# Delta-rule scan of a hybrid layer: key pairs of the state side by side, output terms in two operations a half, the last scan opened for the old block's tiles

## The chip, the cores and the metric

One core of a Trainium2 chip runs the whole kernel. The metric is the device time of one execution in microseconds, the median of several; lower is better.

## The reference

Input x is (2, 1024, 256) in float32. Four sublayers follow each other, each added to its input; LN is a layer norm without weights:

```
x = x + window_attention(LN(x))     # 32 heads of 8, window 128: own and previous block of 128
x = x + ffn(LN(x))                  # 256 -> 1024 relu -> 256, 4-bit weights with scales, plus LoRA
x = x + delta_layer(LN(x))          # below
x = x + ffn(LN(x))                  # the same weights
```

delta_layer, cut to what matters (T = 1024 steps, 32 heads of 8, S is 8 x 8 per head and batch):

```
h = rms(x)
q, k, v = silu(silu(causal_conv4(h @ W.T)))   ; q, k = l2norm(q), l2norm(k) ; beta = sigmoid(h @ Wbeta.T)
for t:  err = S k_t - v_t ;  S = S - beta_t * err k_t^T ;  o_t = S q_t
x = x + rms(o) @ Wout.T ;  x = x + (silu(gate) * up) @ Wdown.T
```

## The kernel before

The 1024 steps are cut into NB = 8 blocks of W = 128 tokens, both batches together. Every engine runs an instruction stream written out by hand as `body(t)` for t = -1 to 8, and waits on semaphores for the others. body(t) holds three blocks at once: the attention, first feed-forward and the delta layer's projections of block n = t+1 (`following`), the scan of block t (`has_scan`), and the tail of block s = t-1 (`tail`: gate_up, mlp_down, ffn_c). `front` is preparation of block n+1 (its queries, keys and score maxima). body(0) has no tail, body(6) no front, body(7) only scan and tail, body(8) only a tail.

**The scan** (VectorE, `scan`, L1180 to L1215). The two batches, 32 heads and two halves of the value rows lie on the 128 partitions; each holds VR = 4 value rows and DK = 8 keys. The block's 128 steps are NC_ = 32 chunks of C = 4. A chunk is four dependent instructions: L1189 multiplies the state by the prepared rows `til` into `first` (a view of `lane_buf`), L1196 sums it to the four steps' updates `u_l`, L1201 multiplies those by the keys into `state[c]`, L1208 sums these products and the old state to the next one. `state` is [NC_+1, VR, DK, C+1]: per value row and key four products and then the state, so states of neighbouring keys lie five floats apart. `between` puts other work of VectorE (score maxima, L1005; attention output scaling, L1037) between the four. The list CUTS has 20, 23 and 24: chunks 0 to 19 run under the attention, 20 to 22 after the second group of maxima, 23 after `first_residual`, and 24 to 31 two at a time after act_of(0) to act_of(3).

**Before the scan** `til_first`, `pair_scale` and `til_column` prepare `til` on VectorE; on GpSimd `pair_rows` (L574) copies the query-key products into `mm_` and `values_til` (L584) the values into `first`; the scan waits for both.

**The output terms** (`terms_of`, L333). o = S q at the start of the chunk plus the chunk's own updates: per step 8 products of state and query and 4 of `mm_` and `u_l`, summed over 12. For 16 chunks that is, for each of four steps, four multiplies by value row (L339) and one for the updates (L340). GpSimd does the first half in `first_terms`, released by the semaphore `scanned`, which VectorE raises after chunk 21, when the room in `lane_buf` is free; VectorE sums them (`first_sums`, L1219), does the second half in `second_terms` between act_of(4) and act_of(5), and sums again (`second_sums`). Then SyncE sends `o_l` to DRAM and back in another layout (L427, L433), ScalarE squares it, TensorE sums the squares, and `output_norm`, `output_product` and `y_of` (L1248) follow.

**Beside it.** On VectorE `first_residual` (L1046), `first_apply` (L986, two scalings of tok), `act_of` (L1256, gate times up, read from PSUM), `second_residual` (L1059, waits for TensorE's ffn_down, L1450), `third_residual` (L1262, waits for mlp_down, L1712), `third_apply`. act_of(i) frees the PSUM tile of gate_up(i+2) (L1703). TensorE runs, per pair, two tiles of ffn_up (L1630) and one of gate_up. ScalarE, in order: 32 exps of the scores (L697), at u=4 the copy of the pair products, at u=16 the copy of attention rows (L705), turn_a(1), y_scale, values_out, turn_c(1) (L663), the norm's root norm_a(1) (L642), a table load, gates 0 to 2 (L816), then relu_a (L743) and the other gates. GpSimd, in order: pair_rows, values_til, first_terms, ffn_bias (L554), ffn_bias_c (L566), residual (L560).

## Time and profile before

| what | value |
|---|---|
| three runs | 1278.09, 1280.63, 1340.21 us; median 1280.63 |
| profiled execution, its own time | 1278.25 us |
| its span, first to last instruction | 1276.4 us |
| mean granted TensorE clock | 0.908 |
| TensorE busy (matmul) | 1060.3 us, 83% |
| VectorE busy | 944.5 us, 74% |
| ScalarE busy | 497.4 us, 39% |
| GpSimd busy | 181.4 us, 14% |
| chain that ended last | TensorE 41%, VectorE 37%, ScalarE 8% |

Busy time is that of executed instructions; waits, semaphores and DMA issues are not in it. The chain is followed back from the last instruction to what released each one. Times in the rows are us from the span's start unless marked ns. A 0.02 to 0.1 us step between two dependent instructions is the semaphore's.

### The profile page before, as it was taken

Reading aid. Unit: us, or ns where it says so; the run is one execution under the profiler, and the core shown is the slowest. Engines: PE = TensorE matmul, PEld = TensorE weight load, DVE = VectorE, ACT = ScalarE, POOL = GpSimd, SP = SyncE. Lnnn points to the kernel's source line nnn. Section 1 sums busy time; section 2 is a strip of 40 time slices with the busy share of each in tenths; the row PEclk is TensorE's granted clock in tenths of the full one; section 3 lists DMA queues with packets and bytes.
Section 4 is the critical chain, followed back from the end, with each engine's and each line's share of the span. In section 5 each row is a group of like instructions: output and inputs, shape, how many; then the busy total and the mean of one; then the engine's idle time right before and its main releaser. Section 6 shows DMA issues by size and latency. Waiting matters only on the chain.

```text
span 1276.4 us, 22025 instructions
## 1 busy us (share of the span) xinstructions
PE 1060.3 (83%) x8600; PEld 723.6 (57%) x8600; DVE 944.5 (74%) x2425; ACT 497.4 (39%) x1027; POOL 181.4 (14%) x251
## 2 busy tenths in 40 slices
PE   3699778777988999989988998899989889932587
PEld 2356545455556755766566655675566547721465
DVE  3824268897889788987888788977897789779611
ACT  2044254326443644345432653364335443610122
POOL 2000000130122010401040013100040004003100
PEclk9579879978998999989988999999999989975788
DMA  9724023203420143013311242024201300110000
GB/s 288 141 46 72 10 75 76 41 1 100 77 41 1 50 111 63 1 34 95 76 21 33 76 82 35 1 75 101 48 2 32 88 2 1 34 58 0 16 9 9
DMA packets 93608, 67.69 MB, mean 53 GB/s; under 512 B 47233, under 2 KB 86337, under 8 KB 93505
## 3 DMA queue, kind: packets, MB, share of 16 engines
q1 hardware_dynamic: 88544, 60.75, 20.1%
q10 hardware_dynamic: 4960, 5.54, 1.6%
q8 instruction: 68, 1.11, 0.4%
q14 instruction: 36, 0.29, 0.1%
HBM read 45.55 MB, written 20.32 MB: 52 GB/s over the span
## 4 chain that ended last, share of the span: by engine, by line
PE 41%; DVE 37%; ACT 8%; DMA 4%; issue 4%; SPq 4%; POOL 1%; DVEq 0%; ACTq 0%; POOLq 0%
PE bank L1558 7%; DVE lane_buf L1189 5%; PE bank L1509 4%; PE bank L1538 4%; DVE state L1208 4%; PE bank L1712 4%; DVE state L1201 4%; DVE u_l L1196 4%; PE bank L1655 3%; PE bank L1543 3%; PE bank L1504 3%; DVE lane_buf L339 2%; DMA q_l<-lane_q 2%; PE bank L1450 2%; DVE mx L1005 2%
## 5 line engine op out<-in xcount | busy, mean ns | idle before, releaser
L697 ACT ACTIVATE probs<-bank 128x512 f32<-128x512 f32 x256 | 152.1, 597 | 200.1 <-PE bank L1543 199.7
L1558 PE MATMUL bank<-probs,v_ext 128*9 128x128 f32 x2048 | 162.0, 279 | 12.1 <-ACT probs L697 6.7
L1005 DVE TENSOR_REDUCE mx<-bank 128x2 f32<-128x320 f32 x256 | 120.9, 486 | 54.3 <-PE bank L1509 49.4
L1703 PE MATMUL bank<-feat_c,wgu 128*128 128x256 f32 (+1 forms) x384 | 96.3, 402 | 57.2 <-DVE hid_c L1256 51.6
L339 POOL TENSOR_TENSOR lane_buf<-state,q_l 128x128 f32<-128x128 f32 x128 | 86.4, 704 | 353.9 <-DVEq L1214 353.9
L1189 DVE TENSOR_TENSOR lane_buf<-state,til 128x128 f32<-128x128 f32 x256 | 109.6, 428 | 17.1 <-POOL lane_buf L584 10.2
L1703 PEld LDWEIGHTS bank<-feat_c,wgu 128*128 128x128 f32 (+1 forms) x384 | 71.1, 190 | 78.1 <-DVE hid_c L1256 55.7
L1558 PEld LDWEIGHTS bank<-probs,v_ext 128*9 128x9 f32 x2048 | 83.5, 91 | 55.1 <-issue 20.3
L1504 PE MATMUL bank<-edge_mask,identb 128*128 128x64 bf16 x512 | 63.1, 208 | 49.8 <-DVE mx L1005 37.6
L1538 PE MATMUL bank<-tri_mask,identb 128*128 128x512 bf16 x256 | 102.1, 399 | 0.5 <-DMA q_stack<-m_rows 0.5
L1543 PE MATMUL bank<-q_stack,k_stack 128*128 128x128 bf16 x1024 | 101.8, 223 | 0.0
L1543 PEld LDWEIGHTS bank<-q_stack,k_stack 128*128 128x128 bf16 x1024 | 81.1, 100 | 33.7 <-issue 4.0
L1509 PE MATMUL bank<-k_stack,q_stack 128*32 128x160 bf16 x2048 | 92.3, 263 | 0.0
L1504 PEld LDWEIGHTS bank<-edge_mask,identb 128*128 128x128 bf16 x512 | 32.8, 101 | 100.3 <-DVE mx L1005 59.7
L1208 DVE TENSOR_REDUCE state<-state 128x32 f32<-128x160 f32 x256 | 81.9, 320 | 7.4
L1196 DVE TENSOR_REDUCE u_l<-lane_buf 128x16 f32<-128x144 f32 x256 | 77.3, 302 | 7.7
L1201 DVE TENSOR_TENSOR state<-u_l,k_l 128x128 f32<-128x128 f32 x256 | 74.8, 292 | 7.2
L1630 PE MATMUL bank<-feat,w_up 128*128 128x256 f32 x256 | 65.6, 406 | 5.4 <-ACT feat L659 5.4
L1726 PE MATMUL bank<-feat_c,w_up 128*128 128x256 f32 x256 | 65.0, 404 | 5.1 <-ACT hid_c L824 3.8
L1083 DVE SCALAR_TENSOR_TENSOR conv<-raw,conv_w,conv 128x256 f32<-128x256 f32 x144 | 63.4, 482 | 2.6
L1726 PEld LDWEIGHTS bank<-feat_c,w_up 128*128 128x128 f32 x256 | 49.6, 201 | 20.7 <-ACT hid_c L824 6.2
L1450 PE MATMUL bank<-w_dn,hid 128*128 128x256 f32 x256 | 57.4, 382 | 4.5 <-ACT hid L743 4.5
(167 smaller groups left out, 1766.1 us busy)
## 6 DMA issues: line engine op xcount, KB each, us to landing
k_pieces<-conv SPq DMA_DIRECT2D x48, 128.0 KB, 2.3
k_stack<-k_pieces SPq DMA_DIRECT2D x32, 192.0 KB
k_stack<-k_pieces SPq DMA_DIRECT2D x32, 128.0 KB
k_l<-lane_k SPq DMA_DIRECT2D x8, 512.0 KB, 3.6
q_l<-lane_q SPq DMA_DIRECT2D x8, 512.0 KB, 5.6
q_pieces<-conv SPq DMA_DIRECT2D x24, 128.0 KB, 2.0
q_stack<-q_pieces SPq DMA_DIRECT2D x32, 96.0 KB
tok<-in_x SPq DMA_DIRECT2D x8, 256.0 KB, 3.2
```

The costliest lines, as they stand in the source:

```text
L697: act.activation(probs[:, u % 2], score_bank[u % 2][:], ACT.Exp, scale=float(DK) ** -0.5).then_inc(exp_done, 1)
L1005: dve.tensor_reduce(mx[:, g, 2 * v:2 * v + 2], bank[1 + u % 2][:, 0:2 * SPAN].rearrange("p (h k) -> p h k", h=2), AX.X, ALU.max).then_inc( ...
L1189: at = mark(dve.tensor_tensor(first[:, c, :, :, 0:DK], state[:, c, :, :, C].rearrange("p v (o k) -> p v o k", o=1).broadcast_to([128, VR, ...
L1196: at = mark(dve.tensor_reduce(u_l[:, c], first[:, c], AX.X, ALU.add))
L1201: at = mark(dve.tensor_tensor(state[:, c, :, :, 0:C], u_l[:, c].rearrange("p v (o i) -> p v o i", o=1).broadcast_to([128, VR, DK, C]), kc[ ...
L1208: at = mark(dve.tensor_reduce(state[:, c + 1, :, :, C], state[:, c], AX.X, ALU.add))
L1504: pe.matmul(edges[:, :, e * W:e * W + SUB], identb[:], edge_mask[:, e * SUB:(e + 1) * SUB].rearrange("p (o s) -> p o s", o=1) .broadcast_t ...
L1509: last = pe.matmul(pb[s * SUB:(s + 1) * SUB, hp * SPAN:(hp + 1) * SPAN], q_stack[:, r, 2 * v + hp, s * SUB:(s + 1) * SUB], keys_of(r, 2 * ...
L1538: pe.matmul(pb[:], identb[:], tri_mask[:].rearrange("p (o t) -> p o t", o=1) .broadcast_to([128, 2, 2 * W]), start=True, stop=False, skip_ ...
L1543: last = pe.matmul(pb[:, at:at + W], keys_of(r, 2 * v + hp)[:, kb * W:(kb + 1) * W], q_stack[:, r, 2 * v + hp, :], start=False, stop=True, ...
L1558: last = pe.matmul(bank[5][row:row + VE, col:col + W], v_ext[:, b, kb, h, :], probs[:, u % 2, (hp * 2 + kb) * W:(hp * 2 + kb + 1) * W], st ...
L1703: last = pe.matmul(late_bank[i % 2][0:m, g * BT:(g + 1) * BT], wgu[:, k, g * INTER + 128 * i:g * INTER + 128 * i + m], fc[:, k], start=(k ...
```

## The change

It lays two keys' groups of the state beside each other (`state` [NC_+1, VR, DK/2, 10]: four products, two states, four products), so that the states of a key pair are neighbours; the four scan instructions keep their sizes, the first one's loops are reordered. `mm_` becomes chunk-major. ScalarE gets two new jobs a block: the queries turned into step-major order (`queries_out`, after exp 16 of the following attention, into the room of `sqk`), and the states of each half copied out densely into `til` (`states_out`: the first half ahead of norm_a(1), the second ahead of gate 5). The output terms of a half become `step_terms` (1024 elements) and `state_terms` (2048): on GpSimd for the first half, on VectorE for the second. `scanned` is raised twice a block. For body(7) VectorE gets `last_scan`, in which act_of, third_residual and third_apply of the old block come between chunks.

```diff
-        mm_ = sb("mm_", [128, C, C, NC_])
+        mm_ = sb("mm_", [128, NC_, C, C])
...
-        state = sb("state", [128, NC_ + 1, VR, DK, C + 1])
-
-        out_terms = lane_buf[:, 0:VR * W // 2 * (DK + C)].rearrange("p (v c i e) -> p v c i e", v=VR, i=C, e=DK + C)
+        state = sb("state", [128, NC_ + 1, VR, DK // 2, 2 * (C + 1)])
+
+        out_terms = lane_buf[:, 0:VR * W // 2 * (DK + C)].rearrange("p (c v i e) -> p c v i e", v=VR, i=C, e=DK + C)
+        q_t = sqk[:].rearrange("p s x -> p (s x)").rearrange("p (c i k) -> p c i k", i=C, k=DK)
+        s_t = til[:].rearrange("p c i k -> p (c i k)").rearrange("p (a x) -> p a x", a=2)[
+            :, :, 0:NC_ // 2 * VR * DK].rearrange("p a (c v k) -> p a c v k", v=VR, k=DK)
...
-        def terms_of(engine, cs, steps=range(C)):
-
-            qc = q_l[:].rearrange("p k (c i) -> p i c k", i=C)
-            n_c = cs.stop - cs.start
-            for i in steps:
-                for v in range(VR):
-                    engine.tensor_tensor(out_terms[:, v, :, i, 0:DK], state[:, cs, v, :, C], qc[:, i, cs, :], ALU.mult)
-                last = engine.tensor_tensor(
-                    out_terms[:, :, :, i, DK:DK + C],
-                    mm_[:, i, :, cs].rearrange("p j (o c) -> p o c j", o=1).broadcast_to([128, VR, n_c, C]),
-                    u_l[:, cs].rearrange("p c v j -> p v c j"), ALU.mult)
-            return last
+        def step_terms(engine, half):
+
+            cs = slice(half * NC_ // 2, (half + 1) * NC_ // 2)
+            return engine.tensor_tensor(
+                out_terms[:, :, :, :, DK:DK + C],
+                mm_[:, cs].rearrange("p c (o i) j -> p c o i j", o=1).broadcast_to([128, NC_ // 2, VR, C, C]),
+                u_l[:, cs].rearrange("p c v (o j) -> p c v o j", o=1).broadcast_to([128, NC_ // 2, VR, C, C]), ALU.mult)
+
+        def state_terms(engine, half):
+
+            cs = slice(half * NC_ // 2, (half + 1) * NC_ // 2)
+            return engine.tensor_tensor(
+                out_terms[:, :, :, :, 0:DK],
+                s_t[:, half].rearrange("p c v (o k) -> p c v o k", o=1).broadcast_to([128, NC_ // 2, VR, C, DK]),
+                q_t[:, cs].rearrange("p c (o i) k -> p c o i k", o=1).broadcast_to([128, NC_ // 2, VR, C, DK]), ALU.mult)
...
-                pool.wait_ge(scanned, n + 1)
-                terms_of(pool, slice(0, NC_ // 2)).then_inc(terms_ready, 1)
+                pool.wait_ge(scanned, n * 2 + 1)
+                step_terms(pool, 0)
+                pool.wait_ge(q_turned, n + 1)
+                pool.wait_ge(s_copied, n * 2 + 1)
+                state_terms(pool, 0).then_inc(terms_ready, 1)
...
-                    last = pool.tensor_copy(mm_[:, i, 0:i + 1, :], pair_l[:, at:at + i + 1, :])
+                    last = pool.tensor_copy(mm_[:, :, i, 0:i + 1].rearrange("p c j -> p j c"), pair_l[:, at:at + i + 1, :])
...
+
+            def queries_out(n, front):
+
+                act.wait_ge(til_ready, n + 1)
+                if front:
+                    act.wait_ge(turned_next, n + 3)
+                act.copy(q_t.rearrange("p c i k -> p k (c i)"), q_l[:]).then_inc(q_turned, 1)
+
+            def states_out(n, half):
+                act.wait_ge(scanned, n * 2 + half + 1)
+                act.copy(s_t[:, half].rearrange("p c v (k e) -> p (c v k) e", e=2),
+                         state[:, half * NC_ // 2:(half + 1) * NC_ // 2, :, :, C:C + 2].rearrange("p c v k e -> p (c v k) e")
+                         ).then_inc(s_copied, 1)
...
+                    if u == QUERIES_AT and after_p:
+                        queries_out(n - 1, front)
...
                 if tail:
                     turn_c(s, 1)
                 if following:
+                    if scan:
+                        states_out(t, 0)
                     norm_a(n, 1)
...
+                if scan and not following:
+                    queries_out(t, False)
...
+                    if following and scan and pair == IT - 4:
+                        states_out(t, 1)
                     if tail and pair < IT - 3:
                         gate_of(s, 3 + pair)
...
+                elif scan:
+                    late(0)
+                    late(1)
+                    states_out(t, 0)
+                    for i in range(2, FT):
+                        late(i)
+                    states_out(t, 1)
...
-                done(dve.tensor_copy(state[:, 0, :, :, C], state[:, NC_, :, :, C]))
+                done(dve.tensor_copy(state[:, 0, :, :, C:C + 2], state[:, NC_, :, :, C:C + 2]))
...
+            def products_of(c):
+
+                whole = state[:, c]
+                return bass.AP(whole.tensor, whole.offset,
+                               [list(whole.ap[0]), [2 * (C + 1) * DK // 2, VR], [2 * (C + 1), DK // 2], [C + 2, 2], [1, C]])
...
                     at = mark(dve.tensor_tensor(
-                        first[:, c, :, :, 0:DK],
-                        state[:, c, :, :, C].rearrange("p v (o k) -> p v o k", o=1).broadcast_to([128, VR, C, DK]),
-                        til[:, c:c + 1, :, 0:DK].broadcast_to([128, VR, C, DK]), ALU.mult))
+                        first[:, c, :, :, 0:DK].rearrange("p v i (k e) -> p i v k e", e=2),
+                        state[:, c, :, :, C:C + 2].rearrange("p v k (o e) -> p o v k e", o=1)
+                        .broadcast_to([128, C, VR, DK // 2, 2]),
+                        til[:, c, :, 0:DK].rearrange("p i (o k e) -> p i o k e", o=1, e=2)
+                        .broadcast_to([128, C, VR, DK // 2, 2]), ALU.mult))
...
                     at = mark(dve.tensor_tensor(
-                        state[:, c, :, :, 0:C],
+                        products_of(c),
                         u_l[:, c].rearrange("p v (o i) -> p v o i", o=1).broadcast_to([128, VR, DK, C]),
-                        kc[:, c:c + 1].broadcast_to([128, VR, DK, C]), ALU.mult))
+                        kc[:, c:c + 1].broadcast_to([128, VR, DK, C]),
+                        ALU.mult))
...
-                    at = mark(dve.tensor_reduce(state[:, c + 1, :, :, C], state[:, c], AX.X, ALU.add))
+                    at = mark(dve.tensor_reduce(state[:, c + 1, :, :, C:C + 2],
+                                                state[:, c].rearrange("p v k (e j) -> p v k e j", e=2), AX.X, ALU.add))
...
                     if (c + 1) * (DK + 1) >= NC_ // 2 * (DK + C) > c * (DK + 1):
                         dve.nop().then_inc(scanned, 1)
+                    if c == NC_ - 1:
+                        dve.nop().then_inc(scanned, 1)
...
-                return dve.tensor_reduce(o_l[:, :, cs], out_terms, AX.X, ALU.add)
+                return dve.tensor_reduce(o_l[:, :, cs].rearrange("p v c i -> p c v i"), out_terms, AX.X, ALU.add)
...
-            def second_terms(i, before):
-                if i == 0:
-                    dve.wait_ge(vstep, before)
-                return mark(terms_of(dve, slice(NC_ // 2, NC_), range(i, i + 1)))
+            def second_steps(before):
+                dve.wait_ge(vstep, before)
+                step_terms(dve, 1)
+
+            def second_states(n):
+                dve.wait_ge(q_turned, n + 1)
+                dve.wait_ge(s_copied, n * 2 + 2)
+                return mark(state_terms(dve, 1))
...
+            def last_scan(t):
+                nonlocal steps
+                steps = 0
+                s = t - 1
+                til_first(t)
+                pair_scale(t)
+                for j in range(C - 1):
+                    til_column(t, j)
+                for i in range(IT):
+                    scan(t, 2 * i, 2 * i + 2, False, False)
+                    act_of(s, i)
+                scan(t, 2 * IT, 2 * IT + 5, False, False)
+                third_residual(s)
+                scan(t, 2 * IT + 5, 2 * IT + 7, False, False)
+                third_apply(s)
+                scan(t, 2 * IT + 7, NC_, False, False)
+                step = first_sums(t)
+                second_steps(step)
+                second_sums(second_states(t))
+                output_norm(t)
+                y_of(t)
+                result(s)
+                dve.sem_clear(vstep)
...
                     act_of(s, 4)
                 if has_scan:
-                    step = second_terms(0, step)
-                    step = second_terms(1, step)
+                    second_steps(step)
                 if tail:
                     act_of(s, 5)
                 if has_scan:
-                    step = second_terms(2, step)
-                    step = second_terms(3, step)
+                    step = second_states(t)
...
-            body(NB - 1, following=False, front=False)
+            last_scan(NB - 1)
             body(NB, has_scan=False, following=False, front=False)
```

## Rows read from the trace of the kernel before

Start and duration are in us; `xN` counts instructions, `128x256 f32` is partitions by elements. POOL is GpSimd, DVE VectorE, ACT ScalarE, PE TensorE.

**Rows 1.** Windows of body(3): us, busy PE, PEld, DVE, ACT, POOL, clock, DMA share, GB/s.
```profile
614.70:639.50 24.80, 24.80 (x358) 14.99 (x356) 21.66 (x72) 11.41 (x20) 0.00 (x0) 1.00 0.34 64
...
647.90:658.20 10.30, 8.77 (x36) 6.66 (x34) 9.46 (x26) 3.62 (x9) 7.36 (x11) 0.89 0.02 4
658.20:682.40 24.20, 22.91 (x120) 18.45 (x120) 23.10 (x60) 7.51 (x15) 8.17 (x12) 1.00 0.00 1
```

**Rows 2.** Timeline of TensorE, body(3): start, duration, work, idle before and its releaser.
```profile
613.68 0.23 PE L1504 MATMUL bank<-edge_mask,identb 128*128 128x64 bf16 x2 [0.93 <-DVE mx L1005]
...
674.62 7.17 PE L1450 MATMUL bank<-w_dn,hid 128*128 128x256 f32 x32 [0.56 <-ACT hid L743]
```

**Rows 3.** Chain that ended last, at second_residual of body(0), body(3) and body(6).
```profile
278.87 0.61 DVE x L1059
...
682.40 0.61 DVE x L1059
...
1085.75 0.61 DVE x L1059
```

**Rows 4.** Instruction groups of VectorE by shape: busy us, mean ns, idle before.
```profile
L1189 DVE TENSOR_TENSOR lane_buf<-state,til 128x128 f32<-128x128 f32 x256 | 109.6, 428 | 17.1 <-POOL lane_buf L584 10.2
L1201 DVE TENSOR_TENSOR state<-u_l,k_l 128x128 f32<-128x128 f32 x256 | 74.8, 292 | 7.2
...
L1219 DVE TENSOR_REDUCE k_l<-lane_buf 128x256 f32<-128x3072 f32 x16 | 53.6, 3349 | 0.3
L339 DVE TENSOR_TENSOR lane_buf<-state,q_l 128x128 f32<-128x128 f32 x128 | 40.7, 383 | 0.0
L340 DVE TENSOR_TENSOR lane_buf<-mm_,u_l 128x256 f32<-128x256 f32 x32 | 19.2, 600 | 0.0
```

**Rows 5.** Instruction groups of GpSimd by shape.
```profile
L339 POOL TENSOR_TENSOR lane_buf<-state,q_l 128x128 f32<-128x128 f32 x128 | 86.4, 704 | 353.9 <-DVEq L1214 353.9
...
L554 POOL TENSOR_TENSOR x_in<-x_in,b_dn 128x256 f32<-128x256 f32 x16 | 11.7, 753 | 123.9 <-DVE tok L986 123.9
...
L560 POOL TENSOR_TENSOR x<-x,z 128x512 f32<-128x512 f32 x8 | 10.2, 1272 | 127.4 <-DVE z L1248 127.4
```

**Rows 6.** Timeline of GpSimd and VectorE side by side, two places.
```profile
650.84 0.66 POOL L339 TENSOR_TENSOR lane_buf<-state,q_l 128x128 f32<-128x128 f32 x1 [47.04 <-DVEq L1214]
650.85 0.82 DVE L1189 TENSOR_TENSOR lane_buf<-state,til 128x128 f32<-128x128 f32 x1
...
733.39 1.36 DVE L1158 TENSOR_TENSOR hid<-u_l,til 128x1152 f32<-128x1152 f32 x1
733.42 1.46 POOL L574 COPY mm_<-u_l 128x96 f32<-128x96 f32 x1
```

**Rows 7.** Timeline of VectorE, first_apply of body(3).
```profile
656.12 1.75 DVE L986 TENSOR_SCALAR tok<-x_in,mv,rstd 128x256 f32<-128x256 f32 x2
```

**Rows 8.** Timeline of ScalarE, body(3).
```profile
619.20 0.60 ACT L697 ACTIVATE probs<-bank 128x512 f32<-128x512 f32 x1 [0.77 <-PE bank L1543]
...
654.63 0.30 ACT L642 ACTIVATE lnv<-mv,eps 128x2 f32<-128x2 f32 x1 [0.31 <-DVE mv L980]
```

**Rows 9.** Instruction group of ScalarE with a strided read.
```profile
L912 ACT COPY wqkv_a<-hid 128x512 f32<-128x512 f32 x2 | 2.1, 1104 | 11.3 <-issue 11.3
```

**Rows 10.** Timeline of VectorE, start of the last scan.
```profile
1136.95 0.38 DVE L1189 TENSOR_TENSOR lane_buf<-state,til 128x128 f32<-128x128 f32 x1 [1.26 <-POOL lane_buf L584]
...
1138.38 0.38 DVE L1189 TENSOR_TENSOR lane_buf<-state,til 128x128 f32<-128x128 f32 x1
```

**Rows 11.** Chain that ended last, after the last scan.
```profile
1193.31 7.50 PE bank L1712 x24
...
1226.59 0.70 DVE z L1248
```

**Rows 12.** DMA issues: KB each, median us to landing.
```profile
lane_o<-k_l SPq DMA_DIRECT2D x8, 256.0 KB, 2.0
q_l<-lane_o SPq DMA_DIRECT2D x16, 128.0 KB, 2.2
```

3 lines of the change are left out of this document (added).

## Prediction

> **What bounds the kernel now.** I read the page first, then the chain of waits, then one middle block, body(3), by windows and timelines, then the end. No engine bounds the whole; the chain changes hands within each block of some 137 us, and an edit is worth what its stretch says. Four stretches matter.
>
> Under the attention TensorE is busy in all of 614.7 to 639.5 [rows 1]; VectorE scans chunks c=0 to 19 beside it. Only at the start does the scan hold it: the first max of the old heads comes after chunk 6, and TensorE stood 0.93 us for it [rows 2].
>
> From 647.9 to 658.2 VectorE is the chain (9.46 of 10.30 us busy, TensorE's clock at 0.89 [rows 1]): chunks 20 to 22, first_residual, chunk 23, first_apply, act_of(0). GpSimd multiplies the first half's output terms at the same time (7.36 us).
>
> From 658.2 to 682.4 two chains run side by side and end almost together. TensorE's, released by act_of(0), runs gate_up, ffn_up and ffn_down without a wait until 674.62 + 7.17 = 681.8 [rows 2]. VectorE's (chunks 24 to 31, sums, output terms) ends at second_residual, 682.4 [rows 3]. So whatever VectorE saves here beyond some 0.5 us, it spends waiting.
>
> In the last scan, body(7), nothing covers VectorE: it starts at 1136.95 [rows 10]; act_of(0) to (5) come after chunks 23 to 31, mlp_down starts at 1193.31, and the old block's tail and then the output path run in series to y_of at 1226.59 [rows 11].
>
> **The first multiply of a chunk.** It takes 384 ns in the middle (mean 428, which holds waits for GpSimd) where one of the same 128 elements with runs of four takes 292 [rows 4]; 0.38 us is what stands at 1136.95 [rows 10]. The old read walks the state five floats apart; the new one reads pairs. Bounds: 0.29 (the run-of-four row) and 0.38 (nothing won). I take 0.29, nearest in kind, since the pair lies together: 0.09 us off a chunk cycle of 1.43 us (1136.95 to 1138.38 [rows 10]), to 1.34. In a middle body only chunks 0 to 6 (0.65 us) and 20, 21 (0.2) count fully on the chain.
>
> The Trainium skill (SBUF — State Buffer, "Door 1: The DMA port swizzle", its box on cachelines) says that accesses within one 16-byte line run at full bandwidth from two hits per line. A pair at floats 4 and 5 of every ten lies in one line, so it would give 0.29 too; no row here shows a run of two.
>
> **Output terms on VectorE (second half).** Out go 16 multiplies of 383 ns and 4 of 600 ns [rows 4], 8.5 us a body. In come one of 1024 and one of 2048 elements. The 3072-element reduction takes 3.35 us, about 1.04 ns an element plus 0.15 [rows 4]: 1.2 + 2.3 = 3.5 us. 5.0 us less, but in bodies 1 to 6 it lies beside ffn_down.
>
> **Output terms on GpSimd (first half).** Out go 16 of about 704 and 4 of about 906 ns, some 14 us. Contiguous products take 753 ns for 256 elements and 1272 for 512 [rows 5]; undisturbed (0.72) that is 2.15 ns an element plus 0.17: step_terms 2.4 us, state_terms 4.6 us. Upper bound: at the strided row's 0.66 us for 128 elements [rows 6], (0.66 - 0.17)/128 = 3.8 ns, state_terms takes 8 us; lower bound, VectorE's 1.04 ns, 2.3 us.
>
> What they do to VectorE matters more. At 650.84 GpSimd starts a product of 0.66 us; VectorE's first multiply, started 0.01 us later, takes 0.82 instead of 0.38: held until 0.44 us into GpSimd's, that is, all but its last 0.22 us. In the other direction a GpSimd copy of 1.46 us spans a VectorE multiply of 1.36 [rows 6]. first_apply's two scalings took 1.75 us [rows 7] with GpSimd active, about 0.74 without. Multiplies with both inputs in SBUF and these scalings are held; reductions and PSUM readers are not. So one long GpSimd product replaces gaps every 0.7 us with one hold of 2.4 - 0.22 = 2.2 us, and one of 4.6 - 0.22 = 4.35 us.
>
> This is also the Trainium skill's rule (SBUF — State Buffer, "Who interferes with whom"): against a GpSimd instruction that reads SBUF, a VectorE one with two SBUF inputs or in a two-port mode waits for the whole of it. It speaks against this change, and the rows agree up to 0.9 us of GpSimd time; none shows a hold of 4 us. By a finer sharing the sum is the first rival's.
>
> Placed in body(3), on the old times: step_terms starts at 650.65 (chunks 20, 21 shorter), so chunk 22's multiply ends at 653.1 instead of 651.7, its chunk at 654.1; first_residual (1.8) ends at 655.95 instead of 654.5. ScalarE's copy of the state comes after its turn, done at 654.3 (654.63 less the idle 0.31 [rows 8]); 0.6 us (its 512 elements of exp take 0.60) to 1.1 (strided read of 512 [rows 9]) puts it at about 655.0. state_terms then runs 655.05 to 659.6 and holds until 659.4, and chunk 23's multiply, due at 655.95, ends at 659.7. Chunk 23 ends at 660.7, first_apply (0.74, now free) at 661.5, act_of(0) at 661.8: 3.6 us later. TensorE's chain is rigid from there: ffn_down ends at 685.4, second_residual stands at 685.45 instead of 682.4, +3.05. VectorE is ready at about 681.8 and waits.
>
> **Queries turned on ScalarE.** 1024 elements after exp 16, ahead of the row copy and of exp 17 (619.20 to 619.80, 0.77 us idle before it [rows 8]). At the contiguous rate 1.0 us; at the strided read's (1104 ns for 512 [rows 9]) 2.05. TensorE needs exp 17 at 620.2: between 0 and 0.9 us of delay, nothing gives it back. The write is strided, so I take 0.7. The second state copy lies before gate 5 (TensorE delivers that later than the scan's end) and costs nothing there; without that cover it would cost its 0.6 us. The pair copies into mm_ on GpSimd become strided writes, but have til_column's 6 us above them.
>
> **Bodies 0 to 6.** Middle body: -0.65 + 3.05 + 0.7 = +3.1, five times: +15.5. Body(0) has no old tail: the state copy is ready early, both GpSimd products run back to back, first_apply ends 4.1 us later; ffn_down then ends at 280.35 and second_residual moves from 278.87 [rows 3] to 280.4, +1.5 (VectorE, rid of 5 us, is no longer last): +1.55 in all. Body(6), second_residual 1085.75 [rows 3]: +2.5 by the same steps, +2.55.
>
> **The last scan.** From 1136.95: 32 x 1.34 = 43.0; six act_of 2.1; third_residual 1.75 and up to 0.9 of waiting for mlp_down (starts 1155.2, 7.50 long [rows 11]); third_apply 0.75; holds 6.3 (2.2 at chunk 22, then its next multiply until state_terms is over) and 0.9 for ffn_bias_c. The scan ends at 1192.6. Sums 3.35, terms 3.5, sums 3.35: 1202.9. The round trip to DRAM, 2.0 + 0.45 + 2.2 [rows 12] and 0.05: 1207.6. Squares 0.6, their sums 1.9, root 0.9, norm 0.8, product 3.8 (sums and product are estimates, twice the 1.0 and 2.0 of the high clock, since TensorE has stood idle): y_of at 1215.6 instead of 1226.59, -11. The old block's tail (ffn_c ends near 1187) is covered. The final 49 us stay.
>
> **Sum.** 15.5 + 1.55 + 2.55 - 11 = +8.6. The profiled execution took 1278.25 us (span 1276.4 and 1.85 around it): 1287. The median shown, 1280.63, is 2.4 us above it, within this error. A difference under 2% (26 us) counts as none, about what a measurement of this kernel can tell.
>
> **Rivals.**
> (A) Long GpSimd products leave VectorE gaps. For: no row shows a long hold, and the saved instructions are real. Against: [rows 6]. Then act_of(0) comes 0.55 us earlier (gate 0 on ScalarE, pushed behind the state copy, stops it at 657.6); middle body -0.65 - 0.55 - 0.5 (the VectorE end) + 0.7 = -1.0, five times -5; body(0), where the VectorE end counts, -4.5; body(6) -1; last scan -11 - 7.2 = -18.2. Sum -29: 1249. Chance 0.22.
> (B) Slower: GpSimd works the short rows of state_terms at its old strided pace, 8 us instead of 4.6. The hold grows by 3.4 us at chunk 23 and nothing covers it: 8 x 3.4 = +27 on mine, 1314. It decides above about 6.6 us (8 x 2.2 = 17 to the 2% line). For: 704 ns for 128 elements; against: the old reads were strided, the new runs are eight and four long. Chance 0.10.
> (C) The pairs win nothing (0.38 stays): 0.85 a body and 2.9 in the last scan, +9: 1296. Against: the run-of-four row. Chance 0.10.
>
> **How the numbers follow.** Mine 0.58 (1275 to 1297). A reaches down to 1240; I cut at 1246, and at 1304 above, where part of B lies beyond: under 0.2 left out. Faster than 1255: A and a little more, 0.24. Slower than 1306: 0.10. Between: 0.66.
>
> **What would show it.** Right: a GpSimd product near 4.6 us in each body, and beside it one first multiply of 3 to 4 us; VectorE idle before second_residual, released by ffn_down; first multiplies at 0.29; last stretch from 1136.95's counterpart to y_of shorter by 11. Wrong: multiplies at 0.29 while state_terms runs (A), state_terms of 7 us (B), 0.38 throughout (C), or a wait for exp 17 well over 1 us.

## The result, and the profile after

The kernel before took 1279.93 us in this comparison (median of 4, 1278.09 to 1340.21), the changed kernel 1292.39 us (median of 4, 1291.68 to 1292.84): a ratio of 1.0109 with a 95% interval of 1.0095 to 1.0123. Ratios here and below are taken over the fast runs alone, without slow ones like that of 1340.21 us. The forecast was 1287 with a range of 1246 to 1304, so the time is slower by 1.1%, inside the range and inside the 2% that count as no change. The profiled spans differ by 13.5 us, 1289.9 against 1276.4.

The page of the changed kernel: busy time of each engine.

```profile
PE 1071.4 (83%) x8593; PEld 732.5 (57%) x8600; DVE 915.4 (71%) x2281; ACT 519.3 (40%) x1051; POOL 114.1 (9%) x107
```

VectorE gave up 29 us of work (944.5 before) and GpSimd 67 (181.4 before), and the kernel is slower. The instruction groups of VectorE, GpSimd and ScalarE by shape (busy us, mean ns, idle before), to be read against [rows 4, 5]:

```profile
L1235 DVE TENSOR_TENSOR lane_buf<-state,til 128x128 f32<-128x128 f32 x256 | 112.4, 439 | 17.0 <-POOL lane_buf L596 10.2
L1249 DVE TENSOR_TENSOR state<-u_l,k_l 128x128 f32<-128x128 f32 x256 | 74.9, 293 | 7.2
...
L350 DVE TENSOR_TENSOR lane_buf<-til,sqk 128x2048 f32<-128x2048 f32 x8 | 18.2, 2276 | 0.0
...
L342 DVE TENSOR_TENSOR lane_buf<-mm_,u_l 128x1024 f32<-128x1024 f32 x8 | 9.7, 1218 | 0.1
```
```profile
L350 POOL TENSOR_TENSOR lane_buf<-til,sqk 128x2048 f32<-128x2048 f32 x8 | 36.5, 4562 | 7.5 <-ACT til L728 7.5
L342 POOL TENSOR_TENSOR lane_buf<-mm_,u_l 128x1024 f32<-128x1024 f32 x8 | 16.2, 2025 | 360.2 <-DVEq L1264 360.2
...
L724 ACT COPY sqk<-q_l 128x1024 f32<-128x1024 f32 x8 | 16.3, 2039 | 0.0
L728 ACT COPY til<-state 128x512 f32<-128x512 f32 x16 | 10.4, 647 | 12.9 <-DVEq L1266 12.2 <-ACT m_rows L703 0.8
```

The first multiply (L1235, formerly L1189) has a mean of 439 ns, no better than the 428 of before [rows 4]. Its own distribution says why (duration min/median/max):

```profile
L1235 DVE TENSOR_TENSOR lane_buf<-state,til x256: 258/292/4221, 203.2 to 1217.1; 128x128 f32<-128x128 f32 x128
```

The usual one takes 292 ns, as forecast; sixteen, two in each body with a scan, take 2.0 to 4.2 us. The timeline of body(3) (start, duration, idle before) shows two of them beside GpSimd's products:

```profile
659.95 2.03 POOL L342 TENSOR_TENSOR lane_buf<-mm_,u_l 128x1024 f32<-128x1024 f32 x1 [46.47 <-DVEq L1264]
659.95 2.17 DVE L1235 TENSOR_TENSOR lane_buf<-state,til 128x128 f32<-128x128 f32 x1
...
662.57 4.60 POOL L350 TENSOR_TENSOR lane_buf<-til,sqk 128x2048 f32<-128x2048 f32 x1 [0.60 <-ACT til L728]
...
664.96 2.36 DVE L1235 TENSOR_TENSOR lane_buf<-state,til 128x128 f32<-128x128 f32 x1
...
669.50 3.35 PE L1781 MATMUL bank<-feat_c,wgu 128*128 128x256 f32 x8 [3.85 <-DVE hid_c L1312]
...
694.76 0.69 DVE L1099 TENSOR_TENSOR x<-bank,x_in 128x512 f32<-128x512 f32 x1 [5.60 <-PE bank L1528]
```

Each held multiply ends with the GpSimd product that it met: 661.98 + 0.14, and 667.17 + 0.15. TensorE then stands 3.85 us for act_of(0)'s tile; before, it stood 0.16 us there in body(3) and 1.9 us in bodies 1, 4 and 5. At the other end VectorE stands 5.60 us at second_residual until ffn_down is over; over the run it is 54.4 us in eight places, 18.9 in two before:

```profile
  PE bank L1528: 54.4, 8
```

Where the 13.5 us are: from til_first to til_first, body(0) took 127.35 us (127.5 before), bodies 1 to 5 took 139.19, 143.31, 139.87, 139.82 and 140.28 (137.34, 136.1, 137.55, 136.27, 136.58), body(6) 128.63 (124.24), and from the last til_first to the end 139.5 (150.1). That is -0.15, +18.6, +4.4 and -10.6 us, and +1.2 us ahead of the first til_first, which starts anywhere from 190.2 to 193.3 us in the thirteen profiles.

The middle bodies by stretch, cut at starts of VectorE's instructions, means of bodies 1 to 5 in us. Every stretch is the difference of two start times in the timelines; "c7" is the first multiply of chunk 7.

| kernel | til_first to c0 | c0 to c7 | c7 to c19 | c19 to c20 | c20 to act_of(0) | act_of(0) to second_residual | to the next til_first | sum |
|---|---|---|---|---|---|---|---|---|
| before | 11.63 | 11.53 | 23.07 | 9.25 | 9.91 | 24.70 | 46.67 | 136.77 |
| changed | 11.71 | 10.91 | 24.36 | 8.68 | 11.86 | 26.22 | 46.76 | 140.49 |
| GpSimd's terms left out (part 1) | 11.65 | 10.91 | 24.36 | 9.35 | 8.55 | 24.12 | 47.50 | 136.44 |
| before + paired states (part 6) | 11.56 | 10.86 | 23.07 | 8.44 | 9.26 | 24.04 | 47.05 | 134.28 |
| before + both (part 6) | 11.71 | 10.87 | 23.33 | 8.92 | 9.28 | 24.36 | 46.82 | 135.28 |

The stretch from c19 to c20 goes by TensorE's granted clock. It is 8.44 or 8.45 us wherever that clock is 1.00 in it, and 9.1 to 9.7 where it is 0.76 to 0.82. That was so in four of the five bodies before, in one of five in the changed kernel and in none with paired states alone; no run shows what decides it.

### The profile page after: what moved, and what is told of

The parts are those of the page before. It is cut to its first block, busy times and chain, and to the rows that moved or that the text cites. A ratio compares the mean times of both kernels' runs of the same rounds, so it can differ in the third digit from the quotient of the medians.

```text
span 1289.9 us, 21787 instructions
## 1 busy us (share of the span) xinstructions
PE 1071.4 (83%) x8593; PEld 732.5 (57%) x8600; DVE 915.4 (71%) x2281; ACT 519.3 (40%) x1051; POOL 114.1 (9%) x107
## 3 DMA queue, kind: packets, MB, share of 16 engines
q8 instruction: 68, 1.11, 0.4%
## 4 chain that ended last, share of the span: by engine, by line
PE 50%; DVE 28%; ACT 11%; SPq 4%; DMA 3%; issue 3%; POOL 1%; DVEq 0%; ACTq 0%; POOLq 0%
PE bank L1636 7%; DVE lane_buf L1235 5%; PE bank L1781 5%; PE bank L1528 5%; PE bank L1708 4%; PE bank L1790 4%; PE bank L1616 4%; PE bank L1587 4%; PE bank L1733 3%; PE bank L1621 3%; DVE state L1257 3%; DVE state L1249 2%; DVE u_l L1244 2%; PE bank L1582 2%; DVE mx L1045 2%
## 5 line engine op out<-in xcount | busy, mean ns | idle before, releaser
L1781 PE MATMUL bank<-feat_c,wgu 128*128 128x256 f32 (+1 forms) x384 | 104.4, 427 | 37.7 <-DVE hid_c L1312 32.1
L1235 DVE TENSOR_TENSOR lane_buf<-state,til 128x128 f32<-128x128 f32 x256 | 112.4, 439 | 17.0 <-POOL lane_buf L596 10.2
L1781 PEld LDWEIGHTS bank<-feat_c,wgu 128*128 128x128 f32 (+1 forms) x384 | 76.4, 204 | 60.5 <-DVE hid_c L1312 35.7
L1582 PE MATMUL bank<-edge_mask,identb 128*128 128x64 bf16 x512 | 62.1, 206 | 43.4 <-DVE mx L1045 29.1
L1249 DVE TENSOR_TENSOR state<-u_l,k_l 128x128 f32<-128x128 f32 x256 | 74.9, 293 | 7.2
L1708 PE MATMUL bank<-feat,w_up 128*128 128x256 f32 x256 | 69.3, 423 | 5.4 <-ACT feat L671 5.4
L1708 PEld LDWEIGHTS bank<-feat,w_up 128*128 128x128 f32 x256 | 52.5, 212 | 19.0 <-ACT feat L671 8.2
```

The lines of the kernel that those rows point to most:

```text
L1235: at = mark(dve.tensor_tensor(first[:, c, :, :, 0:DK].rearrange("p v i (k e) -> p i v k e", e=2), state[:, c, :, :, C:C + 2].rearrange("p ...
L1582: pe.matmul(edges[:, :, e * W:e * W + SUB], identb[:], edge_mask[:, e * SUB:(e + 1) * SUB].rearrange("p (o s) -> p o s", o=1) .broadcast_t ...
L1708: last = pe.matmul(bank[1 + i % 2][:, 0:BT], w_up[:, k, i * 128:(i + 1) * 128], f[:, k], start=(k == 0), stop=(k == KT - 1))
L1781: last = pe.matmul(late_bank[i % 2][0:m, g * BT:(g + 1) * BT], wgu[:, k, g * INTER + 128 * i:g * INTER + 128 * i + m], fc[:, k], start=(k ...
```

## Experiments

Eleven more kernels ran, in three groups. Each group ran on one chip together with the kernel before, so kernels of different groups are best compared by their ratios. "Held" is what VectorE's two multiplies of a chunk (the first one, and the one that writes the products) took beyond the 74.9 + 74.8 us that they take where GpSimd computes no terms: 112.4 + 74.9 - 149.7 = 37.6 us in the changed kernel. first_apply's scalings, which are held as well, are not in it: they take 5.9 us in the changed kernel, 8.8 in those with cut state terms in their old place, and 13.0 in the kernel before.

| kernel | median us | ratio to before (95%) | held, us |
|---|---|---|---|
| changed kernel | 1292.4 | 1.0109 (1.0095 to 1.0123) | 37.6 |
| GpSimd's terms left out | 1249.9 | 0.9776 (0.9756 to 0.9796) | 0 |
| 12 products of 256 elements | 1253.4 | 0.9811 (0.9789 to 0.9833) | 8.2 |
| only the state terms cut, 8 x 256 | 1265.6 | 0.9911 (0.9883 to 0.9938) | 20.1 |
| state terms in 2 x 1024 | 1281.6 | 1.0037 (1.0019 to 1.0056) | 33.9 |
| state terms after first_apply | 1286.5 | 1.0061 (1.0041 to 1.0081) | 45.5 |
| queries' copy in 4 | 1294.4 | 1.0118 (1.0080 to 1.0157) | 45.0 |
| before + paired states | 1258.9 | 0.9846 (0.9832 to 0.9861) | 11.1 |
| before + open last scan | 1267.8 | 0.9917 (0.9901 to 0.9934) | |
| before + both | 1249.9 | 0.9781 (0.9763 to 0.9799) | |
| products cut, queries' copy cut | 1247.4 | 0.9764 (0.9749 to 0.9779) | 10.4 |
| the same, state terms after first_apply | 1243.5 | 0.9737 (0.9721 to 0.9753) | 9.9 |

**1. What do GpSimd's two products cost?**

```diff
                 pool.wait_ge(scanned, n * 2 + 1)
-                step_terms(pool, 0)
...
-                state_terms(pool, 0).then_inc(terms_ready, 1)
+                pool.nop().then_inc(terms_ready, 1)
```

> The changed kernel, in which GpSimd computes neither the step terms nor the state terms of the first half, and only signals that they are there; so the output terms of the first half of every block are not computed. Everything on VectorE, ScalarE and TensorE is as in the changed kernel. Theory 1 (GpSimd's two whole products of 2.0 and 4.6 us hold VectorE's multiplies with two operands in SBUF, 2.0 and 2.1 us a body): in the middle bodies act_of(0) comes 2.1 us earlier, TensorE waits less for it and runs ffn_down's first units at the higher clock, together some 3 to 4 us a body; body(0) and body(6) about the same, the last body, where the scan has nothing to hide behind, some 7 us, as its first sums also wait for GpSimd's terms. Sum 25 to 45 us, the time 1248 to 1268 us, and no L1235 of about 4.2 or 2.2 us is left. Rival (the lengthening comes from ScalarE's two copies or from the scan's own lines, and the holds lie in time that VectorE would have waited in anyway): under 10 us, 1283 us or more.

Measured 1249.88 us, 42 less than the changed kernel. The first multiply in its groups of VectorE by shape:

```profile
L1234 DVE TENSOR_TENSOR lane_buf<-state,til 128x128 f32<-128x128 f32 x256 | 74.9, 293 | 17.0 <-POOL lane_buf L595 10.2
L1248 DVE TENSOR_TENSOR state<-u_l,k_l 128x128 f32<-128x128 f32 x256 | 74.8, 292 | 7.2
```

37.6 us of held multiplies are gone, and 42 us of time. ScalarE's two copies ran here as in the changed kernel, so they are not what costs the 42. The table by stretch says where it lies: a middle body loses 3.3 us from c20 to act_of(0), where the holds are, and 2.1 behind act_of(0), where TensorE restarts at a lower clock; 1.4 comes back in the other stretches.

**2. Is it GpSimd's work or the length of one product?**

```diff
-                step_terms(pool, 0)
+                for lo in range(0, NC_ // 2, 4):
+                    step_terms(pool, 0, lo, lo + 4)
...
-                state_terms(pool, 0).then_inc(terms_ready, 1)
+                for lo in range(0, NC_ // 2, 2):
+                    last = state_terms(pool, 0, lo, lo + 2)
+                last.then_inc(terms_ready, 1)
```

> The changed kernel with GpSimd's step terms of the first half in 4 instructions of 4 chunks each and its state terms in 8 instructions of 2 chunks each, 256 elements apiece, instead of one of each. The same elements are computed. Theory 1 (a VectorE multiply waits for the end of the GpSimd product that it meets, so the length of one product is the cost): a meeting then costs at most 0.6 us instead of 2.2 to 4.3, and the time falls by 15 to 30 us, to 1262 to 1277 us; the longest L1235 is under 1.2 us. Rival A (the port passes back and forth and each of the 12 short products holds one VectorE multiply, so the sum of the holds is as before): 1288 us or more, with the same total of VectorE's time on L1235, in more and shorter holds. Rival B (holds are not the cause): no change, 1290 to 1295.

Measured 1253.41 us, below the range expected. GpSimd's groups and VectorE's first multiplies in this kernel:

```profile
L350 POOL TENSOR_TENSOR lane_buf<-til,sqk 128x256 f32<-128x256 f32 x64 | 47.2, 771 | 0.4
L342 POOL TENSOR_TENSOR lane_buf<-mm_,u_l 128x256 f32<-128x256 f32 x32 | 20.6, 672 | 357.8 <-DVEq L1267 357.8
```
```profile
L1238 DVE TENSOR_TENSOR lane_buf<-state,til 128x128 f32<-128x128 f32 x256 | 81.8, 319 | 17.0 <-POOL lane_buf L599 10.2
...
L1252 DVE TENSOR_TENSOR state<-u_l,k_l 128x128 f32<-128x128 f32 x256 | 76.1, 297 | 7.2
```

GpSimd is now busy for 67.8 us with the same elements (52.7 as two products), and the kernel is 39 us faster. What counts is the length of one instruction, not GpSimd's total. The longest first multiply of the run took 0.81 us; the chunk's reductions, which aren't held (302 ns in the mean with GpSimd's terms and without), run in between.

**3. How does the price go with the length?** Two halves for the state terms, step terms whole; then step terms whole, state terms in eight.

```diff
-                state_terms(pool, 0).then_inc(terms_ready, 1)
+                for lo in range(0, NC_ // 2, 8):
+                    last = state_terms(pool, 0, lo, lo + 8)
+                last.then_inc(terms_ready, 1)
```

> The changed kernel with GpSimd's state terms of the first half in 2 instructions of 8 chunks (1024 elements, about 2.3 us each) instead of one of 4.6 us; the step terms stay one instruction of 2.0 us. Theory 1 (a VectorE multiply that begins while a product of GpSimd runs waits for that product's end, so a product much longer than the 1.3 us of a chunk catches a multiply for all that is left of it; one of 0.8 us catches little): three products of 2.0 to 2.3 us still hold VectorE for 1 to 2 us each, 3 to 6 us a body against 4.7 in the changed kernel, and the time is 1278 to 1294 us, far above the 1253 us of the kernel in 256-element pieces. Rival (any cut lets the multiplies in between, and the price follows the longest product): half of the gain, 1268 to 1276 us. Rival (what the 12 pieces gained came from something else than their length, such as the later end of the terms): cannot be far from 1253.

```diff
-                state_terms(pool, 0).then_inc(terms_ready, 1)
+                for lo in range(0, NC_ // 2, 2):
+                    last = state_terms(pool, 0, lo, lo + 2)
+                last.then_inc(terms_ready, 1)
```

> The changed kernel with GpSimd's state terms in 8 instructions of 256 elements, and its step terms still in one of 1024 elements (2.0 us). Theory 1 (each long product has its own hold, about 2.1 us for either): with only the step terms' hold left, half of the 39 us comes back: 1268 to 1278 us, and a L1235 of about 2.2 us once in each body. Rival (only the state terms' hold delays act_of(0), the earlier one is made up in waits that follow): 1253 to 1258 us.

Measured 1281.63 and 1265.58 us. VectorE's groups of the kernel with halves:

```profile
L1237 DVE TENSOR_TENSOR lane_buf<-state,til 128x128 f32<-128x128 f32 x256 | 96.8, 378 | 17.0 <-POOL lane_buf L598 10.2
L1251 DVE TENSOR_TENSOR state<-u_l,k_l 128x128 f32<-128x128 f32 x256 | 86.8, 339 | 7.2
```

Halves save little: the second half catches the chunk's other multiply (L1251, 12 us more than undisturbed), since a product of 2.4 us is still longer than a chunk. Pieces of 0.8 us, shorter than a chunk's 1.3 us, leave 8.2 us of holds, and no first multiply over 0.81 us. No length between 0.8 and 2.0 us was run, so that the chunk's own length is the limit is argued, not shown. The step terms alone, 2.0 us long, cost 12 us (1265.6 us with them whole, 1253.4 with them cut too; held 20.1 and 8.2). Over the five kernels of parts 1 to 3, the time above the one without terms (0, 3.5, 15.7, 31.8, 42.5 us) rises with the held time (0, 8.2, 20.1, 33.9, 37.6), though not in proportion.

**4. The place of a hold.**

```diff
                 pool.wait_ge(s_copied, n * 2 + 1)
+                if n < NB - 1:
+                    pool.wait_ge(tok_ready, (n + 1) * 3 + 2)
                 state_terms(pool, 0).then_inc(terms_ready, 1)
```

> The changed kernel in which GpSimd's state terms of the first half wait until VectorE has normed the next block's first activations (first_apply), so that their 4.6 us lie in the last chunk of the scan instead of ahead of it. Theory 1: the hold of 2.2 us ahead of first_apply is gone and act_of(0) comes 2 us earlier, but act_of(1) or the chunk between them is held instead; TensorE's eight ffn_down units of 0.38 to 0.48 us cover part of that. Net 0 to 2 us a body, the time 1278 to 1292 us, best guess 1286. Rival (what matters is how much GpSimd holds in all, not where): no change, 1291 to 1294. Rival (the step terms' hold alone is what delays): 1290 to 1294 also, but with first_apply not earlier.

Measured 1286.49 us. The product and the multiply that it held, on the timeline of body(3):

```profile
664.99 4.53 POOL L350 TENSOR_TENSOR lane_buf<-til,sqk 128x2048 f32<-128x2048 f32 x1 [5.21 <-DVE tok L1028]
...
665.49 4.18 DVE L1237 TENSOR_TENSOR lane_buf<-state,til 128x128 f32<-128x128 f32 x1
```

This is nearly the full hold of 4.35 us that the prediction spoke of: the multiply began 0.50 us into the product and ended 0.15 after it. VectorE was held for 8 us more in all (45.5 against 37.6) and the kernel was still 6 us faster, because the hold stands after the tile that TensorE waits for: from c20 to act_of(0) the middle bodies take 10.25 us in the mean instead of 11.86, and from there to second_residual 27.08 instead of 26.22.

**5. ScalarE's copy of the queries.**

```diff
-QUERIES_AT = 16
+QUERIES_AT = (26, 27, 28, 29)
...
-                act.copy(q_t.rearrange("p c i k -> p k (c i)"), q_l[:]).then_inc(q_turned, 1)
+                for a in parts:
+                    last = act.copy(q_t.rearrange("p c i k -> p k (c i)")[:, 2 * a:2 * a + 2], q_l[:, 2 * a:2 * a + 2])
+                    if a == 3:
+                        last.then_inc(q_turned, 1)
```

> The changed kernel with ScalarE's transposed copy of the queries (1024 elements, 2.0 us, ahead of attention's exponential 16) in 4 copies of 256 elements, ahead of exponentials 26 to 29. Theory 1 (the copy is longer than TensorE's lead over ScalarE in attention, and costs 1.3 us of the exponentials' sequence in each of 7 bodies): each short copy is hidden or costs a quarter, so 3 to 9 us less, 1283 to 1289 us, and the exponentials 16 to 19 take 4.6 us again as in the kernel before. Rival (the exponentials wait for TensorE anyway, and the copy is hidden as a whole): no change, 1291 to 1294. Rival (strided short copies cost as much each and hit a tighter place): slower, up to 1298.

A miss: 1294.38 us, no gain. In body(3) the stretch did get shorter: the matmuls behind exponential 17 stand 26.42 us after til_first, 27.60 in the changed kernel. The windows of body(3), from til_first in stretches of 24, 26, 12 and 31 us and the rest (busy PE, PEld, DVE, ACT, POOL, clock, DMA share, GB/s), show it given back. First the changed kernel, then the one with the cut copy:

```profile
651.77:663.77 12.00, 10.18 (x99) 7.51 (x100) 10.68 (x27) 3.46 (x9) 3.23 (x2) 1.00 0.25 35
663.77:694.77 31.00, 25.91 (x115) 20.61 (x117) 23.80 (x53) 10.17 (x20) 4.86 (x3) 0.94 0.00 1
```
```profile
651.14:663.14 12.00, 10.57 (x79) 7.55 (x71) 10.07 (x26) 3.04 (x9) 2.02 (x1) 0.72 0.12 15
663.14:694.14 31.00, 26.01 (x98) 20.41 (x99) 25.60 (x51) 10.68 (x21) 5.96 (x3) 0.83 0.00 0
```

TensorE's granted clock fell from 1.00 and 0.94 to 0.72 and 0.83, and VectorE's holds rose to 45.0 us. The two hang together. From c7 to c19 all five middle bodies of this kernel take 23.07 us, 1.29 less than the changed kernel, so the cut copy did its work. But in bodies 3 to 5 the clock from 50 to 62 us after til_first is 0.72. There TensorE delivers the tile of ScalarE's turn later (in body(3) the turn stands at 662.43, 61.3 us after til_first; 59.5 in the changed kernel), ScalarE's copy of the states follows it, and GpSimd starts state_terms just ahead of chunk 23's multiply:

```profile
663.70 4.51 POOL L350 TENSOR_TENSOR lane_buf<-til,sqk 128x2048 f32<-128x2048 f32 x1 [2.81 <-ACT til L732]
663.88 4.48 DVE L1239 TENSOR_TENSOR lane_buf<-state,til 128x128 f32<-128x128 f32 x1
```

That multiply takes 4.4 to 4.5 us in bodies 3 to 5, and 2.0 to 2.4 in bodies 1 and 2, where the clock of that window is 1.00. Why the clock fell in these bodies and not in those of the changed kernel no run shows. So the same edit was tried on top of the cut products.

> The changed kernel with both edits: GpSimd's 12 products of 256 elements for the first half, and the copy of the queries in 4 copies of 256 elements ahead of exponentials 26 to 29. With the products cut, the copy's cost shows in the trace of that kernel: in body(3) the matmuls behind exponential 17 stand 1.4 us later against til_first than in the kernel before with paired states alone. Theory 1 (that 1.4 us goes through to the end once nothing in VectorE is later; in the kernel with only the copy cut it was given back to a lower TensorE clock in front of act_of(0)): 5 to 10 us less than 1253 us in 6 to 7 bodies, 1243 to 1248 us. Rival (the stretch is given back at act_of(0) or at the tensor clock here too): 1251 to 1256 us.

Measured 1247.44 us: 6 us less than the 1253.41 of part 2 (ratios 0.9764 and 0.9811). The place itself can be seen by comparing the kernel of part 2 with the one of part 6 that has no such copy; ScalarE and TensorE in body(3), first with the copy, then without:

```profile
612.71 2.04 ACT L727 COPY sqk<-q_l 128x1024 f32<-128x1024 f32 x1
614.54 0.63 ACT L720 COPY tok_c<-bank 128x512 f32<-128x512 f32 x1
...
615.32 0.29 PE L1639 MATMUL bank<-probs,v_ext 128*9 128x128 f32 x2 [1.21 <-ACT tok_c L720]
```
```profile
609.96 0.58 ACT L707 COPY tok_c<-bank 128x512 f32<-128x512 f32 x1
...
611.21 0.29 PE L1569 MATMUL bank<-probs,v_ext 128*9 128x128 f32 x2
```

With til_first at 587.62 and 584.92, these matmuls stand at 27.70 and 26.29: 1.41 us, of which 0.14 stands there already at the first chunk. From c7 to c19 the middle bodies take 24.35 to 24.57 us in the mean of every profile with the whole copy, and 23.07 to 23.33 in those without it or with it cut: 1.3 us for the copy, where the prediction had 0.7. The wait that ends last isn't exponential 17 but the row copy behind it (tok_c), whose bank the next matmuls need.

**6. The other two parts alone, on the kernel before.** One has `last_scan(NB - 1)` in place of `body(NB - 1, following=False, front=False)`, with last_scan as in the change but for the output terms:

> The kernel before with one change: its last body with a scan runs VectorE in the changed kernel's order (the old block's tiles between the chunks of the scan, no waits for a next block). The layout of the states, the output terms and the queries stay as they were. Theory 1 (the reordering is worth what the prediction put on it, apart from the other parts: VectorE's old-block tiles go where it idled): 11 to 18 us less, 1260 to 1269 us. Rival (half of the 11 us that the last stretch lost came from the shorter output terms and multiplies): 3 to 8 us less, 1270 to 1277 us.

Measured 1267.81 us, 10.6 less; from the last til_first (1125.63) to the end of the span (1266.0) it is 140.4 us, 150.1 before. The other has the paired states only:

```diff
-        state = sb("state", [128, NC_ + 1, VR, DK, C + 1])
+        state = sb("state", [128, NC_ + 1, VR, DK // 2, 2 * (C + 1)])
```

with the four instructions of a chunk as in the change, and output terms that read the pairs in place.

> The kernel before with one change: the states of two keys side by side, with the first multiply (0.38 us) writing and reading pairs; output terms still in 80 short instructions, last body in the old order. Theory 1 (the first multiply falls to 0.29 us, which VectorE gains in every body, but in the middle bodies TensorE's ffn_down is the later one by the gate in hand, so only body(0), body(6) and the last body gain, 2.9 us each at the most, plus 0.2 to 0.6 us in each middle body): 6 to 11 us less, 1267 to 1273 us. Rival (VectorE's lead time turns into time in every body, 8 x 2.9 us): 1255 to 1260 us. Rival (the gain is lost in the other three instructions of the chunk, which now read and write two keys at a stride): 1276 to 1281 us.

Measured 1258.85 us, 19.6 less: a miss, against 6 to 11 expected. It is about twice what the prediction's rival C gave it, and lies inside the range of the second theory, "VectorE's lead time turns into time in every body". The number fits that theory and the trace does not: the chunks beside the attention gained nothing (part on the prediction, below). Body(0) fell by 3.6 us, body(6) by 2.2, the last stretch by 3.6, and the middle bodies from 136.8 to 134.3 in the mean. The gate, TensorE's first units behind act_of(0):

```profile
648.73 1.99 PE L1714 MATMUL bank<-feat_c,wgu 128*128 128x256 f32 x8 [1.24 <-DVE hid_c L1267]
```

It stands 63.81 us after til_first; before it was 66.62. Of these 2.8 us, 1.0 lies from c19 to c20 and 0.5 ahead of the first chunk. Then both together:

> The kernel before with two of the three parts: states of two keys side by side, and the last body in the changed kernel's order. Output terms, their 40 short instructions on each of GpSimd and VectorE, and the untransposed queries stay. Theory 1 (the parts add: -19.6 and -10.6 us from 1278.4): 1246 to 1251 us. Then the third part, the output terms in two operations a half, costs 41 to 46 us as it was made, and still 3 to 7 us with its products cut on GpSimd. Rival (the parts overlap in the last body, whose multiplies count in both): 1251 to 1256 us, and the third part with cut products costs nothing.

Measured 1249.91 us, 27.2 less by the medians of that comparison, 28 by the ratio, against 30.2 for the sum: the parts add within 3 us. The bodies 1 to 5 of this kernel are those of the one with paired states alone, but they took 135.3 us in the mean here (granted clock of the run 0.910) and 134.3 there (0.920), so 1 us of the 2.5 differs from one profile to the next: bodies 1, 3 and 5 of the second profile have 9.21 to 9.24 us from c19 to c20 at a clock of 0.79, the others 8.44 and 8.45 at 1.00. The third part, output terms in two operations a half with copied states and turned queries, therefore costs 1.0109 - 0.9781 = 0.033 of 1278, 42 us, as it was made.

**7. The pieces put in their place.** Products cut, queries' copy cut, and the eight pieces of the state terms behind first_apply (the wait of part 4):

> As the kernel with both edits (12 products on GpSimd, 4 copies of the queries), and GpSimd's 8 pieces of the state terms wait until first_apply is done, except in the last body. Theory 1 (the short products still hold VectorE's multiplies for 1.0 us ahead of act_of(0) in body(3) of the kernel with cut products, of which some 0.5 us belongs to the pieces of the state terms; what they hold after act_of(0) hides beside ffn_down): 0 to 4 us less than that kernel, best guess 2 us. Rival (GpSimd's terms become the late ones at first_sums, or TensorE's clock takes the gain): 0 to 5 us more.

Measured 1243.53 us, ratio 0.9737 (0.9721 to 0.9753): 49 us less than the changed kernel and 34 less than the one before. It is 6.4 us below the kernel with paired states and open last scan alone, so the third part, so mended, is worth something: body(0) 121.2 against 124.2 us, body(6) 120.7 against 122.2, the last stretch 133.5 against 136.1, but bodies 1 to 5 the same within 0.2 us in the mean.

## Why the prediction was right, and what in it was wrong

The mechanism, a long GpSimd product that holds VectorE's multiply ahead of the gate, is right and shown by parts 1 to 4. That the total, 1287 against 1292.4, comes so near is partly luck, since two wrong sizes cancelled: the hold ahead of act_of(0) and the clock behind it.

- **The first multiply**, 0.38 to 0.29 us: right, median 292 ns. The Trainium skill's note on 16-byte cachelines (SBUF — State Buffer, the box under "Door 1: The DMA port swizzle") is borne out: a run of two floats in one line costs what a run of four does, 292 ns. No run laid a pair across two lines.
- **What it is worth in a middle body**: "In a middle body only chunks 0 to 6 (0.65 us) and 20, 21 (0.2) count fully" held in its first half. From c0 to c7 it is 0.6 to 0.7 us less in the mean wherever the states are paired, and the chunks beside the attention gain nothing: c7 to c19 takes 23.07 us with and without pairs, since TensorE has no gap there. The first multiplies of chunks 7, 19 and 20 in body(3), before and with paired states alone:

```profile
615.37 0.38 DVE L1189 TENSOR_TENSOR lane_buf<-state,til 128x128 f32<-128x128 f32 x1
...
638.43 0.37 DVE L1189 TENSOR_TENSOR lane_buf<-state,til 128x128 f32<-128x128 f32 x1
...
647.87 0.38 DVE L1189 TENSOR_TENSOR lane_buf<-state,til 128x128 f32<-128x128 f32 x1
```
```profile
607.48 0.28 DVE L1197 TENSOR_TENSOR lane_buf<-state,til 128x128 f32<-128x128 f32 x1
...
630.55 0.28 DVE L1197 TENSOR_TENSOR lane_buf<-state,til 128x128 f32<-128x128 f32 x1
...
639.00 0.29 DVE L1197 TENSOR_TENSOR lane_buf<-state,til 128x128 f32<-128x128 f32 x1
```

  What was priced too small is the rest. The pairs alone gave 2.5 us a middle body in one profile: 0.7 from c0 to c7; 0.65 from c20 to act_of(0), where chunks 22 and 23 count too; 0.7 behind act_of(0), where VectorE's end was the later one by 0.5 us (24.51 to second_residual in bodies 2 to 5 before, 24.04 with pairs), which rival C left out; and 0.8 from c19 to c20, at a higher clock. 0.4 is given back behind second_residual. The clock's part is not shown to come from the pairs, as it was there in only two of the five middle bodies of the other kernel with pairs. The windows from 50 to 62 us after til_first, before and with paired states:

```profile
641.64:653.64 12.00, 11.05 (x90) 7.67 (x90) 9.62 (x28) 2.33 (x7) 2.80 (x5) 0.72 0.21 27
```
```profile
634.92:646.92 12.00, 10.57 (x85) 8.10 (x86) 10.56 (x34) 4.31 (x11) 5.14 (x9) 1.00 0.12 14
```

- **GpSimd's products**: 2.4 and 4.6 us forecast, 2.03 and 4.56 measured. Rival B, 8 us, is out.
- **The holds**: the mechanism right, one size wrong. "one hold of 2.4 - 0.22 = 2.2 us" measured 2.17 - 0.29 = 1.88. The other was to be met 0.9 us in, for 3.5 us of waiting at chunk 23; in body(3) the multiply met it 2.4 us in and waited 2.36 - 0.29 = 2.07. ScalarE's copy of the states came right behind its turn, as forecast, but the turn stood 59.5 us after til_first; the prediction had taken 62.1 from the body(3) before (653.74), whose clock was 0.72 in that window, and it was 1.00 now:

```profile
661.29 0.58 ACT L675 COPY feat_c<-bank 128x512 f32<-128x512 f32 x1 [0.79 <-PE bank L1508]
661.77 0.65 ACT L728 COPY til<-state 128x512 f32<-128x512 f32 x1
```

  So state_terms began 0.60 us behind step_terms, not 2.0, and first_residual ran beside it. Where the clock was low, in the kernel of part 5, the hold was nearly the whole product (4.48 - 0.29 = 4.19), and so it was in the last scan, where the multiply took 4.22 us.
- **act_of(0) and TensorE behind it**: the holds were to put act_of(0) off by 3.6 us; from c20 to act_of(0) it was 1.95 (9.91 to 11.86). From there to second_residual the sum had -0.5 us, since TensorE's chain was called rigid; it was +1.2 in bodies 3 to 5 and +3.7 in body(2). These are the two wrong sizes: a hold too long by 1.65 us and a clock term put at nothing, worth 2.0 in the mean. In body(3), first_apply stands 66.6 us after til_first, 64.5 before, and after standing 3.85 us TensorE ran its first eight units in 3.35 us instead of 1.99. What that clock costs is read from these rows; no run held it fixed. In body(2) it was worse, and that body is the long one (+7.2 us):

```profile
527.54 3.78 PE L1781 MATMUL bank<-feat_c,wgu 128*128 128x256 f32 x8 [3.84 <-DVE hid_c L1312]
531.12 1.06 PE L1508 MATMUL bank<-ident,tok 128*128 128x128 f32 x4
532.85 3.78 PE L1708 MATMUL bank<-feat,w_up 128*128 128x256 f32 x8 [0.68 <-ACT feat L671]
```

- **VectorE's saving at the output terms** is hidden in bodies 1 to 6: right. 8.5 us became 2.28 + 1.22 = 3.5, and it all turned into waiting for ffn_down (5.60 us in body(3)). The kernel of part 7 is ahead of the one without the third part only in body(0), body(6) and the last stretch, which fits.
- **The queries' copy**: 2.05 us forecast, 2.04 measured; its cost 1.3 instead of 0.7 a body.
- **The sum**, forecast against measured: middle bodies +15.5 against +18.6, body(0) +1.55 against -0.15, body(6) +2.55 against +4.4, the last stretch -11 against -10.6, and 1.2 us at the start that no step had. A middle body was +3.1 against +3.7. The measured one is made of -0.6 (c0 to c7), +1.3 (the queries' copy), +1.95 (holds), +1.5 (behind act_of(0)), -0.6 (c19 to c20 at the higher clock, which no step had) and +0.2 elsewhere.
- **Rival A**, the same kernel with no long hold, was put at 1249 us; leaving GpSimd's terms out gave 1249.9 and short products 1253.4. That 1249.9 meets 1249 is partly luck: by the profile with the terms left out, body(6) was worth -4.3 instead of -1, and the last stretch -15.9 instead of -18.2. **Rival C** put the pairs at 9 us; alone they are worth 19.6, so its price was too small by half, for the reasons given above.

What stays open: how much of the 42 us of GpSimd's products is clock and how much hold. The stretches put 3.3 us a middle body ahead of act_of(0) and 2.1 behind it, but the holds themselves make TensorE wait before its clock falls, and no run fixed the clock. Open is also what sets the clock between c19 and c20.

## What to carry to other kernels

Before GpSimd's short instructions are joined into one long one, look at what VectorE does beside it: a VectorE multiply with both inputs in SBUF waits for the end of the GpSimd product that it meets, so here 256-element pieces, 29% more GpSimd time in all, beat whole products by 39 us, and two pieces of 2.4 us for the state terms won only 11 us; pieces shorter than the neighbour's own cycle (0.8 against 1.3 us here) are the ones that paid. If a long instruction can't be cut, put it behind the tile that the bounding engine waits for. When a saving is priced by stretches, count the end of each stretch too: here the chunks beside a gapless TensorE were rightly put at nothing, but half a microsecond at the next gate was left out. And read more than one body before taking a position from it: the turn that started GpSimd's product stood 58 to 62 us after til_first with the granted clock, and the length of the hold went with it (the held multiply took 2.0 to 2.4 or 4.4 to 4.5 us).
